# Inverse standard deviation from integer bits and Newton steps on VectorE, in the attention stage of a two-layer transformer

## What is computed

```python
def _layernorm(x, axis=-1, eps=1e-05):
    m = jnp.mean(x, axis=axis, keepdims=True)
    v = jnp.var(x, axis=axis, keepdims=True)
    return (x - m) / jnp.sqrt(v + eps)

x = x + tanh(g_xattn[0]) * retention(_layernorm(x), ctx, ctx)         # decayed sum of ctx*ctx, times q
x = x + tanh(g_ffn[0])   * moe0(_layernorm(x), Wg, W_in, W_out)       # top 2 of 8 experts, gelu
x = x + tanh(g_xattn[1]) * attention(_layernorm(x), ctx, ctx, ...)    # masked softmax, 128 keys a block
x = x + tanh(g_ffn[1])   * moe1(_layernorm(x), gate_w, w1, w2)        # top 2 of 8 experts, silu
```

## Time and profile before

| | before |
|---|---|
| median of three runs | 646.42 us (644.92 to 647.86) |
| the profiled execution | 642.86 us |
| its span, first to last instruction | 641.1 us |
| PE / PEld / DVE / ACT / POOL busy | 546.8 / 489.0 / 334.0 / 322.5 / 233.7 us |
| mean granted TensorE clock | 0.911 |
| table loads on ScalarE (all lines) | 13, of 1.283 us each |
| ScalarE roots of norms 2 and 3 | 8, of 0.296 us mean |

### The profile page before, as it was taken

How to read it: one execution, slowest core, us unless ns; L and a number is a source line. 1 busy time by engine, 2 the same in 40 slices (tenths; PEclk the granted TensorE clock), 3 DMA queues, 4 the chain that set the end, 5 groups by cost and what they waited for, 6 DMA issues and landing times.

```text
span 641.1 us, 12043 instructions
## 1 busy us (share of the span) xinstructions
PE 546.8 (85%) x3565; PEld 489.0 (76%) x3566; DVE 334.0 (52%) x810; ACT 322.5 (50%) x643; POOL 233.7 (36%) x260
## 2 busy tenths in 40 slices
PE   4897669699999999887777229999999999999991
PEld 2467458699999999855666228898999889889891
DVE  2563953446566665368854764455453544453530
ACT  3495233446666666347774314456454555544540
POOL 3300156335444533355000114354354445354441
PEclk9896787989999999988885559999999999999997
DMA  8923024324534534343014005444452445263221
GB/s 277 373 85 131 2 59 155 114 78 135 162 85 168 172 108 140 107 144 121 33 67 164 1 18 157 108 99 105 107 163 41 128 106 146 38 164 49 33 37 23
DMA packets 51091, 70.59 MB, mean 110 GB/s; under 512 B 6832, under 2 KB 42928, under 8 KB 51056
## 3 DMA queue, kind: packets, MB, share of 16 engines
q1 hardware_dynamic: 40352, 50.04, 23.9%
q0 software_dynamic: 10704, 20.10, 14.1%
HBM read 49.80 MB, written 20.33 MB: 109 GB/s over the span
## 4 chain that ended last, share of the span: by engine, by line
PE 66%; DVE 12%; issue 7%; ACT 5%; DMA 4%; POOL 2%; SPq 1%; DVEq 1%; POOLq 0%; ACTq 0%
PE PA L1392 22%; PE PD L1392 18%; PE PC L1392 7%; PE PD L1267 5%; PE PC L1553 3%; PE PC L1267 3%; DVE ys L937 2%; PE PB L1261 2%; DMA out<-ys,row_o 2%; DVE xs L1071 2%; PE PB L1404 1%; ACT xn L589 1%; DVE wlo L1057 1%; DVE stats L855 1%; PE PB L1535 1%
## 5 line engine op out<-in xcount | busy, mean ns | idle before, releaser
L1392 PE MATMUL PD<-whi,hhi 128*128 128x256 f32 x420 | 122.9, 293 | 0.0
L1392 PE MATMUL PD<-whi,hlo 128*128 128x256 f32 x420 | 118.8, 283 | 0.0
L1392 PE MATMUL PD<-wlo,hhi 128*128 128x256 f32 x420 | 118.8, 283 | 0.0
L543 POOL DMA_INDIRECT out<-ys,row_o x35 | 55.8, 1595 | 104.1 <-DVE ys L1214 103.2
L1392 PEld LDWEIGHTS PD<-wlo,hhi 128*128 128x128 f32 x420 | 80.5, 192 | 0.0
L1392 PEld LDWEIGHTS PD<-whi,hhi 128*128 128x128 f32 x420 | 80.3, 191 | 0.1
L1392 PEld LDWEIGHTS PD<-whi,hlo 128*128 128x128 f32 x420 | 80.3, 191 | 0.0
L813 ACT ACTIVATE hhi<-PC 128x512 fp32r<-128x512 f32 x70 | 38.1, 596 | 67.5 <-PE PC L1553 67.5
L467 POOL DMA_INDIRECT y_rows<-ys,row_y x40 | 41.8, 1045 | 67.2 <-ACT ys L686 65.7
L808 ACT ACTIVATE xT<-PA 128x512 f32<-128x512 f32 x72 | 42.2, 597 | 47.5 <-PE PA L1392 47.2
L1392 PE MATMUL PA<-whi,xhi 128*128 128x512 f32 x144 | 60.3, 419 | 2.6 <-DVE xlo L1057 2.6
(11 more groups left out here) (233 smaller groups left out, 1345.8 us busy)
## 6 DMA issues: line engine op xcount, KB each, us to landing
raw<-w SPq DMA_DIRECT2D x16, 1024.0 KB, 5.6
raw<-L_ffn_W_in SPq DMA_DIRECT2D x8, 1024.0 KB, 5.7
raw<-L_ffn_W_out SPq DMA_DIRECT2D x8, 512.0 KB, 3.5
y_rows<-ys SPq DMA_DIRECT2D x8, 512.0 KB, 8.2
xn_rows<-xn SPq DMA_DIRECT2D x8, 512.0 KB, 3.4
xs<-x SPq DMA_DIRECT2D x4, 512.0 KB, 6.1
cx<-ctx SPq DMA_DIRECT2D x4, 512.0 KB, 6.8
ys<-y_rows SPq DMA_DIRECT2D x4, 512.0 KB, 4.6
```

Of the source, the lines that this page charges most:

```text
L543: pool.indirect_dma_start(out, bass.IndirectOffsetOnAxis(ap=row_o[:, j:j + 1], axis=0), ys[:, j % 2, :], None, compute_op=ALU.add).then_in ...
L1392: mm = pe.matmul(dst, a[k], b[k], start=(first and k == 0 and a is lhs_hi and b is rhs_hi), stop=(last and k == n - 1 and a is lhs_lo))
```

## The change

For n = 2 and 3 ScalarE's `root` does nothing any more: its wait, its root instruction and the semaphore `sd_ready` are gone. VectorE's `coefs` doesn't wait for it. In place of the reciprocal it adds epsilon to the variance in place, shifts the bits of the float right by one as an integer, subtracts that from the constant 0x5F375A00 (the first guess), and makes three Newton steps of three instructions each. That is twelve linked instructions on 128x4 tiles (the variance is read and written at every second element) in place of one. The tables `mv`, `sd`, `rstd` and `nmr` get a place for each quad of norm 2 as well, so 10 places and not 7. Norms 0 and 1 are as before.

```diff
+RSQRT = 0x5F375A00
...
-        mv = sb("mv", [P, 3 + NQ, QB, 2])
-        sd = sb("sd", [P, 3 + NQ, QB])
-        rstd = sb("rstd", [P, 3 + NQ, QB])
-        nmr = sb("nmr", [P, 3 + NQ, QB])
+        mv = sb("mv", [P, 2 + 2 * NQ, QB, 2])
+        sd = sb("sd", [P, 2 + 2 * NQ, QB])
+        rstd = sb("rstd", [P, 2 + 2 * NQ, QB])
+        nmr = sb("nmr", [P, 2 + 2 * NQ, QB])
...
-            return n + (q if n == 3 else 0)
+            return n if n < 2 else 2 + (n - 2) * NQ + q
...
             def root(n, q):
+                if n >= 2:
+                    return
                 act.wait_ge(var_ready, VAR[n, q])
...
             def coefs(n, q):
 
-                dve.wait_ge(sd_ready, VAR[n, q])
                 m = place(n, q)
-                link(dve.reciprocal(rstd[:, m, :], sd[:, m, :]))
+                if n < 2:
+                    dve.wait_ge(sd_ready, VAR[n, q])
+                    link(dve.reciprocal(rstd[:, m, :], sd[:, m, :]))
+                else:
+                    guess, step, var = rstd[:, m, :], sd[:, m, :], mv[:, m, :, 1]
+                    bits = guess.bitcast(I32)
+                    link(dve.tensor_scalar(var, var, LN_EPS, None, ALU.add))
+                    link(dve.tensor_scalar(bits, var.bitcast(I32), 1, None, ALU.arith_shift_right))
+                    link(dve.tensor_scalar(bits, bits, -1.0, float(RSQRT), ALU.mult, ALU.add))
+                    for _ in range(3):
+                        link(dve.scalar_tensor_tensor(step, guess, -0.5, guess, ALU.mult, ALU.mult))
+                        link(dve.tensor_tensor(step, step, var, ALU.mult))
+                        link(dve.scalar_tensor_tensor(guess, step, 1.5, guess, ALU.add, ALU.mult))
                 link(dve.scalar_tensor_tensor(nmr[:, m, :], mv[:, m, :, 0], -1.0, rstd[:, m, :], ALU.mult, ALU.mult))
                 dve.sem_inc(coef_ready, 1)
```

## The result

The changed kernel takes 660.68 us (median of four runs, 659.9 to 661.44) where the kernel before takes 646.83 (four runs, 644.92 to 647.86). The ratio is 1.0213, with a 95% interval of 1.018 to 1.0247: 13.9 us slower. The forecast was 657.8 us, 11.4 slower, in a range of 654.0 to 661.5.

The account below looks back on a forecast made before the run. The attention stage was taken as bound by the path from statistics through coefficients to normalised rows. 3.9 + 4.4 - 1.28 + (4.4 - 0.6) + 1.93 - 1.36 gave 11.4 us on 646.42: 657.8 us, range 654.0 to 661.5.

Parts of the forecast that it names:

- The price of an instruction: VectorE's linked instructions in a set: 0.200 us each for nine and 0.206 for three, 2.42 us for the twelve.
- A set that had waited for the root: Coefficients on VectorE: 0.13 + 2.42 - 0.62 = 1.93 us more for a norm that used to wait for ScalarE's root.
- Quads 0 and 1: Norm 2's first two sets: 1.93 us each, 3.86 late, carried as 3.9 to VectorE's adding of quad 0's attention.
- The two sets ahead of quad 3's rows: VectorE's `coefs(3, 0)` and `coefs(2, 3)`, both roots ready before: 2 x 2.20 us more, rows 8.3 us late.
- The load that comes back: ScalarE's table load at 319.04 us, behind quad 3's rows of norm 2, is gone: -1.28 us, exponentials 7.0 us late.
- Norm 3: End of the stage: 4.4 - 0.6 us for two sets, 1.93 for the last, less 1.36 of slack; 11.4 us late.
- TensorE's clock: Quad 0's scores at the lower clock would take 1.8 us more, of which 0.1 at most is on the path.
- My sign of being wrong: Wrong if the step were under 0.1 us, PE's stage pieces grew longer, or the second expert layer's time changed.
- the first: Added instructions fall into VectorE's room or cost far less than 0.2 us each; 643 us at price zero; chance 0.03.
- The second: The low clock spreads over PE's quad 3 scores, quad 2 values and turns: 14 to 15 us, 661 us; chance 0.12.
- The third: The compiler puts loads elsewhere: 12.7 us, 659 us, chance 0.04; or rounding moves a token between experts, chance 0.01.
- The fourth: Hidden in part, such as the last 2.0 us if quad 3's rows come just in time: 656 us; chance 0.10.

Follow-up runs that it names:

- a_reorder: The changed kernel with VectorE taking the coefficients of norm 2's quad 3 ahead of norm 3's quad 0; 1.0205 times before, 13.2 us above it.
- newton_n3: The kernel before with Newton coefficients for norm 3 alone, norm 2 keeping ScalarE's root; 1.0108 times before, 7.0 us above it.
- steps2: The changed kernel with two Newton steps in place of three, nine instructions in a set; 1.0115 times before, 7.4 us above it.
- steps5: The changed kernel with five Newton steps in place of three, eighteen instructions in a set; 1.0353 times before, 22.8 us above it.
- after: The changed kernel's first profile, three Newton steps for norms 2 and 3 against the kernel before; the profiled execution took 660.62 us.
- a_again: The changed kernel, unchanged, with a second profile; 1.0214 times before, and the profiled execution took 660.43 us.

## Why the prediction was right, step by step

- **The price of an instruction** was 0.198 us and not 0.202, in the six sets where GpSimd rests. In busy time the forecast's own terms give 14.5 us more on VectorE, and 15.3 came. The long instructions add 2.6, and the combine of quad 2 gives 1.6 back (2.58 us for 4.17), as GpSimd's share is over by then; that lies off the path.
- **A set that had waited for the root**: forecast 1.93 us more. Quad 2 of norm 2: `nmr` starts 312.71 - 310.17 = 2.54 us after the statistics end, forecast 2.55. Quad 3 of norm 3: 18.40 - 16.50 = 1.90 more. Right.
- **Quads 0 and 1**: forecast 3.9 us up to VectorE's adding of quad 0's attention. Measured: 316.31 - 307.46 = 8.85, less the 1.74 that the stage began late, 7.1 us. This is the term that was mis-sized. I had priced the twelve instructions from rows where GpSimd rests, and put them beside its share of the combine and its value bias: 2.2 us in quad 1's set and 0.4 in quad 0's, both shown by the pair without that work. Another 0.7 is the scores of quad 1 at the lower clock for longer (309.18 to 314.29 us, before 301.05 to 305.46, from their start to the next product's).
- **The two sets ahead of quad 3's rows**: forecast 4.40, measured 330.14 - 316.95 = 13.19 less the 8.85 that their first instruction was late, 4.34. That it holds in either order was learned from `a_reorder`.
- **The load that comes back**: forecast -1.28, measured 11.78 - 13.19 = -1.41. A switch costs the load and no more: the one that is left starts at 305.41, lasts 1.28, and the exponentials go on at 306.70. By the further 1.38 us of drain in the Trainium skill ("ScalarE: Activation LUTs", section "What ACT_TABLE_LOAD costs") the forecast would have been 10.0 us, further off than the 11.4 by the row.
- **Norm 3**: forecast 11.4 - 7.0 = 4.4 from the statistics of quad 2 to the end of the stage. Measured 16.92 - 12.73 = 4.2 us. `newton_n3` alone has 7.0 us with the early set's 2.2 in it, forecast 6.5.
- **TensorE's clock**: given 0.1 us on the path. It was 0.7 at quad 1's scores and 0.9 at the turn of quad 3's rows, which I had only in a rival. My sign of being wrong, that PE's pieces in the stage grow longer, did come.
- **The sum** for the first pair of profiles closes: 7.1 + 4.3 - 1.4 + 0.9 + 4.2 = 15.1, measured 15.2. Of the 3.8 above the forecast 2.6 is GpSimd and 1.6 the clock, and the other terms came out 0.4 below it together. The clock's part isn't the change's alone, as the kernel before loses 1.8 us around the same places in its second profile. Against the mean of both, the excess is 2.3 us, and the medians say 2.5.

Of the rivals, the first (the instructions fall into VectorE's room) is refuted by `steps2` and `steps5`: the room is there, 59.3 us busy of 85, and a set still costs by its count of instructions. The second happened in a small part. The third didn't: the loads went. The fourth didn't either: quad 3's rows of norm 3 came late enough to hold up the copy, by 16.94 us at 361.75 where the copy of quad 1 was 15.05 late. The forecast fell 2.5 us short of 13.9; the median lies inside the range but near its upper end. The range held because it was wide enough for the two terms that were too small, not because they were foreseen.

## What to carry to other kernels

Short linked instructions on a 128x4 tile cost 0.2 us each, however little they do, so twelve of them are dearer than a trip to another engine and back (0.62 us) and a table load (1.28 us) together. Before trading loads for arithmetic, count the loads that something waits for: here it was two of the seven that went, and hiding them instead brought nothing that could be measured. And price the new instructions from rows where the same neighbour is at work: beside GpSimd single ones lasted up to 0.58 us in place of 0.17, and the set 4.8 us in place of 2.5.

## What the runs showed of the hardware that I had not expected

- A VectorE instruction of 128x4 elements, 0.17 us alone, can last 0.46 to 0.58 us while GpSimd runs a tensor_tensor of 128x256 or 128x1024. Forms with one tensor input and with two were both held up. In `after`, `a_again` and `steps5` all 22 long ones of the sets of quads 0 and 1 end 0.02 us behind the end of a GpSimd instruction. So the price goes by what is left of GpSimd's instruction, and not by the tiny tile.
- The compiler gave Ln and Exp two tables, and loaded one after the other sixteen times in the stage.
- The stage varies by 1.8 us between two executions of one kernel, along with TensorE's granted clock (0.93 and 0.76 from 315 to 338 us).
